# Tail of a routed feed-forward kernel: the threshold search with two small operations a bit, five bits in two pairs, and finding rounds of four tiles

## The chip, the cores and the metric

One core of one Trainium2 chip. The metric is the device time of one execution in microseconds (us), as the median of the timed runs.

## The reference, cut to what matters

A vision transformer, a memory layer and a routed feed-forward layer follow each other. The change is in the last one:

```python
T = Bn * Sn                                   # 64 * 229 = 14656 tokens of D = 128
logits = jnp.einsum('gsd,de->gse', xg, gate_w)          # E = 16 experts
probs = jax.nn.softmax(logits, axis=-1)
flat_probs = probs.transpose(2, 0, 1).reshape(En, T)
scores, tok_idx = jax.lax.top_k(flat_probs, cap)        # cap = T / E = 916 tokens an expert
toks = xf[tok_idx]
h = jax.nn.gelu(jnp.einsum('ecd,edh->ech', toks, w1) + b1[:, None, :])
y = jnp.einsum('ech,ehd->ecd', h, w2) + b2[:, None, :]
y = y * scores[..., None]
routed = jnp.zeros_like(xf).at[tok_idx.reshape(-1)].add(y.reshape(-1, Dn))
shared = jax.nn.gelu(xf @ sw1 + sb1) @ sw2 + sb2
out = (routed + shared).reshape(Bn, Sn, Dn)
```

## The kernel before, in words

The kernel is a row of phases; `tail_phase` is the last and the only one touched. It handles 32 pairs of sequences (PAIRS, the shared feed-forward on all tokens) and then 32 units (two for each of 16 experts, UNITS). Every engine runs one list of instructions written out by hand, with n from 0 to 63 for pair or unit, and semaphores between the lists.

**The main loop.** TensorE (PE) does for each n: `up(n+1)` (L1600 to L1612, four products of 458 columns into the banks U, each of them two passes of fp32) and `down(n)` (L1614 to L1625, 16 products of 128 columns into bank O). ScalarE (ACT) applies the gelu between them (L1714) and issues the output transfers of the shared part. VectorE (DVE) adds in `total_of(n)` (L1807 for pairs, L1815 and L1818 for units). GpSimd (POOL) adds the bias sb2 to h for each pair (L1784), and after that issues the indirect transfers.

**Routing.** At the start the DVE takes the softmax of the router's logits (L1932 to L1942, the exponential on ACT at L1735), PE turns the probabilities (L1642) and the DVE copies them to `prob` (L1948), 128 partitions of 1832 values, eight partitions for each expert. SP loads ten constants first (L1561), and PE, ACT, POOL and DVE each wait for all ten (`load` at 160) before their first work in the tail.

**The search.** The 916th largest probability of every expert is found bit by bit, 30 bits. For a bit, `search` (L1821 to L1828) forms a candidate `cand = thr | bit` (L1824) and counts the values at or over it (L1827, with an accumulator output); PE's `count` sums the counts of an expert's partitions into bank C (L1651); `settle` (L1830 to L1836) keeps the bit where the sum reaches 916 (L1832, L1835) and shifts the bit (L1836). Two bits go with each pair n = 1 to 15: PE issues up(n+1), count, down(n), count. Then `chosen` (L1842, L1843, a scan at L1848), `ranked` at n = 16 and `placed` at n = 17 turn the threshold into running counts `runx`, which SP writes to memory and reads back as `run64` (L1571, L1577).

**The finding.** For expert e, at n = 19 + e, `one_hot(e)` (L1890, L1893) builds rows that select for each slot its block of tokens; `find` (PE, L1664) multiplies them with the running counts, one round for two tiles of 120 slots, into bank C or X by turns; `tokens` (DVE, L1902 to L1913) subtracts the start from the slot in two steps, counts within the block (L1908, two tiles), and adds the token's base in two steps. There are four rounds an expert. PE's order is up(n+1), rounds 0 and 1, `turn_x` (L1633, from n = 30 on: the transposes of a later unit's tokens, in bank X, which wait for all rounds found so far), down(n), rounds 2 and 3. The DVE's order is tokens of rounds 0 and 1, total_of(n), tokens of rounds 2 and 3, one_hot of the next expert. So one_hot(e+1) stands behind the last round of e, and the first round of e+1 waits for it.

**Gather and scatter.** POOL gathers the rows of the first 12 experts (AHEAD) from `table`, eight transfers each (L1757), each pair of them as soon as its token indices are there. Then it runs `scatter(e)` for e = 0 to 15 (L1768, eight transfers with addition, the first four after y of unit 2e, the others after unit 2e+1), with four more gathers behind each of the first eight. The scatters of an expert wait until all those of the one before have landed. y has four buffers.

Of the kernel before, what the change touches and what calls it, by code (L numbers as in the profile page):

```python
# [12 lines left out]
F32 = mybir.dt.float32  # L13
BF16 = mybir.dt.bfloat16
I32 = mybir.dt.int32
# [869 lines left out]
WL = 2 * L  # L885
# [594 lines left out]
LAST_BIT = FIRST_BIT + BITS // 2 - 1  # L1480
# [4 lines left out]
def tail_phase(nc, g, A, out):  # L1485

    UNITS = 2 * E
    with ExitStack() as ctx:
        s = Sems(nc, ctx, "load ew0 ew1 gel_pad eb2 bias b_part up gelu down sum0 sum1 sent0 sent1 "
                 "r_max r_sub r_exp r_sum r_inv r_prob r_turn r_copy scored table "  # L1490
                 "t_set t_cand t_count t_total t_step t_thr t_bit t_gt t_tie t_pref t_off t_need t_sel t_run t_runoff "
# [24 lines left out]
        thr, bit, cand, step = (sb(n, [128, 1], I32) for n in ("thr", "bit", "cand", "step"))  # L1516
# [4 lines left out]
        local, inside, junk = sb("local", [XL, 2]), sb("inside", [XL, 2]), sb("junk", [XL, 2, BLK])  # L1521
# [17 lines left out]
        X, C = (ctx.enter_context(nc.psum_tensor(n, [128, 512], F32)) for n in ("z_X", "z_C"))  # L1539
        summed, sent = [s["sum0"], s["sum1"]], [s["sent0"], s["sent1"]]  # L1540
# [15 lines left out]
        with nc.Block() as block:  # L1556
            @block.sync
            def _(sp):
                for dst, src in ((sw1, "sw1"), (sw2, "sw2"), (sb1, "sb1"), (sb2, "sb2"), (eb1, "eb1"), (same, "same_expert"),
                                 (ahead, "ahead"), (slot, "slot"), (order, "order"), (base, "base")):  # L1560
                    sp.dma_start(dst[:], A[src]).then_inc(s["load"], 16)  # L1561
# [37 lines left out]
            def _(pe):  # L1599
                def up(n):  # L1600
# [4 lines left out]
                    for k in range(4):  # L1605
# [8 lines left out]
                def down(n):  # L1614
# [5 lines left out]
                    for t in range(4):  # L1620
# [4 lines left out]
                    mm.then_inc(s["down"], 1)  # L1625
# [27 lines left out]
                def find(e, r, turned):  # L1653
# [391 lines left out]
```

## Time and profile before

| | us |
|---|---|
| median of 3 runs | 3929.04 (3922.57 to 3930.95) |
| the profiled execution, its own time | 3925.95 |
| its span in the profile | 3924.1 |
| mean granted clock of TensorE | 0.949 of full speed |
| the tail | from 3223.7 to 3924.1 |

The profile is one execution. Times in rows are us from the start of its span. PE is the matmul, PEld the weight load, and a fp32 product shows as two rows. A row of the timeline gives start, length, engine, line, operation, tiles, number of instructions merged, and in brackets the idle time before it with what ended it. A merged row of matmuls ends some tenths after the next row starts, since the ends are modelled.

### The profile page before, as it was taken

What the parts mean: (1) busy time and instruction counts of PE and PEld (TensorE: products, weight loads), DVE (VectorE), ACT (ScalarE), POOL (GpSimd) and SP (SyncE); (2) the same over time, 40 slices, a digit from 0 to 9 for tenths busy, and PEclk for the clock granted to TensorE, in tenths of its full rate; (3) what the DMA queues carried; (4) which work ended last, traced back from release to release, by engine and by line L of the source; (5) the groups of instructions that cost most, each with busy time, mean ns of one, the idle gap of its engine ahead of it and who ended that gap; (6) DMA issues with size and microseconds to landing.
All of it is one profiled execution on the core that took longest, in us unless ns stands there. A gap on an engine that the chain in (4) does not pass through costs nothing. (4 is left out here: it accounts for less than half of the span.)

```text
span 3924.1 us, 88868 instructions
## 1 busy us (share of the span) xinstructions
PE 3456.2 (88%) x29756; PEld 2634.2 (67%) x29756; DVE 2496.5 (64%) x6387; ACT 1917.9 (49%) x3500; POOL 2285.1 (58%) x2633
## 2 busy tenths in 40 slices
PE   7899999889999889999988999996997879867973
PEld 4577787667877667787766777774445656645762
DVE  2267776567777556777655777666986878765110
ACT  0156666346666436666534666654653433211331
POOL 0356663756664475666365666455985643364876
PEclk9999999889999989999988999998998989988997
DMA  6856663146665036666214666501111222221432
GB/s 223 244 112 125 129 132 59 26 85 124 132 130 110 8 59 118 131 129 127 50 36 80 130 128 129 104 2 33 34 27 41 62 63 36 59 72 35 74 58 29
DMA packets 456054, 342.03 MB, mean 87 GB/s; under 512 B 70659, under 2 KB 440171, under 8 KB 455595
## 3 DMA queue, kind: packets, MB, share of 16 engines
q1 hardware_dynamic: 404419, 275.69, 35.9%
q10 hardware_dynamic: 24224, 46.44, 3.7%
q0 software_dynamic: 27136, 16.42, 3.1%
q8 instruction: 150, 2.46, 0.3%
q14 instruction: 125, 1.02, 0.1%
HBM read 227.69 MB, written 109.29 MB: 86 GB/s over the span
## 5 line engine op out<-in xcount | busy, mean ns | idle before, releaser
L730 DVE TENSOR_REDUCE a_neg_max<-a_S 99x4 f32<-99x788 f32 x1024 | 1003.6, 980 | 499.1 <-PE a_S L319 495.3
L528 ACT ACTIVATE a_shared<-a_St 99x792 f32<-99x792 f32 (+1 forms) x1024 | 850.3, 830 | 622.0 <-PE a_St L336 610.4
L319 PE MATMUL a_S<-a_k_st,a_q_st 96*99 96x197 bf16 x4096 | 546.8, 256 | 46.8 <-DVE a_neg_max L730 46.5
L319 PEld LDWEIGHTS a_S<-a_k_st,a_q_st 96*99 96x99 bf16 x4096 | 395.1, 127 | 265.3 <-DVE a_neg_max L730 226.6
L336 PE MATMUL a_St<-a_q_st,a_k_st 99*99 99x198 bf16 (+1 forms) x4096 | 523.4, 250 | 47.0 <-DMA a_q_st<-a_max_rows 31.8
L355 PE MATMUL a_O<-a_shared,a_v_aug 99*32 99x198 f32 (+1 forms) x8192 | 461.3, 337 | 0.6
L336 PEld LDWEIGHTS a_St<-a_q_st,a_k_st 99*99 99x99 bf16 (+1 forms) x4096 | 386.6, 125 | 76.8 <-DMA a_q_st<-a_max_rows 39.2
L355 PEld LDWEIGHTS a_O<-a_shared,a_v_aug 99*32 99x32 f32 (+1 forms) x8192 | 246.1, 109 | 82.9 <-ACT a_shared L528 1.3
L673 POOL TENSOR_TENSOR h<-h,a_rows 99x512 f32<-99x512 f32 x128 | 163.1, 1274 | 213.0 <-DVE a_shared L805 213.0
L641 POOL CAST a_max_parts<-a_neg_max 99x32 bf16<-99x32 f32 x128 | 26.8, 210 | 446.6 <-DVE a_neg_max L730 446.6
L659 POOL CAST a_parts<-a_q_k 128x792 bf16<-128x792 f32 x128 | 107.8, 843 | 306.7 <-issue 261.3
L468 PEld LDWEIGHTS a_O<-a_w,a_shared 128*99 128x99 f32 x2048 | 245.6, 168 | 46.3 <-issue 29.9
L468 PE MATMUL a_O<-a_w,a_shared 128*99 128x128 f32 x2048 | 267.7, 275 | 3.5 <-DVE h L828 3.5
L594 ACT ACTIVATE a_shared<-a_St,a_cols 128x396 f32<-128x396 f32 x256 | 150.9, 591 | 238.9 <-PE a_St L479 230.5
L1768 POOL DMA_INDIRECT out<-h,token x128 | 210.3, 1643 | 96.9 <-DVE h L1818 41.8
L828 DVE TENSOR_TENSOR h<-a_O,h 99x512 f32<-99x512 f32 x128 | 88.5, 692 | 226.7 <-PE a_O L468 226.7
L661 POOL TENSOR_TENSOR a_q_k<-a_q_k,a_parts 128x792 f32<-128x792 f32 x128 | 216.0, 1687 | 10.3
L665 POOL TENSOR_TENSOR a_parts<-a_q_k,a_parts 128x792 bf16<-128x792 f32 x128 | 215.7, 1685 | 10.3
L479 PE MATMUL a_St<-a_shared,a_w 128*128 128x396 f32 x512 | 208.3, 532 | 2.5 <-ACT a_shared L600 2.5
L1714 ACT ACTIVATE z_gel<-z_U,z_sb 128x458 f32<-128x458 f32 x128 | 80.5, 643 | 223.1 <-PE z_U L1611 188.0
L1815 DVE TENSOR_TENSOR h<-z_O,xT 120x512 f32<-120x512 f32 x32 | 22.1, 689 | 235.0 <-DMA out<-h,token 174.7
L1714 ACT ACTIVATE z_gel<-z_U,z_eb 128x458 f32<-128x458 f32 x128 | 81.5, 642 | 184.3 <-PE z_U L1611 169.6
(266 smaller groups left out, 7473.9 us busy)
## 6 DMA issues: line engine op xcount, KB each, us to landing
a_shared<-in_x ACTq DMA_DIRECT2D x64, 594.0 KB, 5.1
spill_q<-a_parts SPq DMA_DIRECT2D x384, 99.0 KB
spill_k<-a_parts SPq DMA_DIRECT2D x384, 99.0 KB
a_k_st<-spill_k SPq DMA_DIRECT2D x128, 297.0 KB
a_q_st<-spill_q SPq DMA_DIRECT2D x128, 297.0 KB
a_k_st<-spill_k SPq DMA_DIRECT2D x128, 198.0 KB
a_q_st<-spill_q SPq DMA_DIRECT2D x128, 198.0 KB
a_k_st<-spill_k SPq DMA_DIRECT2D x128, 99.0 KB
```

What stands on the lines that cost most here:

```text
L319: mm = nc.tensor.matmul(S[0:TC, j // 2, j % 2 * TB:j % 2 * TB + NTOK], q_st[p % 4][0:SPLIT, head, b * TB + c * TC:b * TB + (c + 1) * TC], ...
L336: mm = nc.tensor.matmul(St[0:keys, j // 2, j % 2 * TB:(j % 2 + 1) * TB], k_st[p][:, head, first:first + keys], q_st[p][:, head, b * TB:(b ...
L355: mm = nc.tensor.matmul(O[32 * j:32 * j + 32, half * TB:(half + 1) * TB], v_aug[p % 4][0:keys, 2 * b + c, half * 4 + j, :], probs[0:keys, ...
L468: mm = nc.tensor.matmul(O[0:TC, t * D:(t + 1) * D], gl[k % 2][:, h, t * TC:(t + 1) * TC], m.w2[:, h * D:(h + 1) * D], start=(h == 0), stop ...
L479: nc.tensor.matmul(St[:, h, 0:PW], m.w1[:, h * 128:(h + 1) * 128], m_yT[n % 2], start=True, stop=True).then_inc(s["m_fc1"], 1)
L528: nc.scalar.activation(probs[0:keys, u % 4, :].rearrange("p (x t) -> p x t", x=2), St[0:keys, :, 0:2 * TB], ACT.Exp).then_inc(s["probs"], 1)
L661: nc.gpsimd.tensor_tensor(q_k[:], q_k[:], parts[:, 0, :, :], ALU.subtract).then_inc(s["res"], 1)
L665: nc.gpsimd.tensor_tensor(parts[:, 2, :, :], q_k[:], parts[:, 1, :, :], ALU.subtract).then_inc(s["lo"], 1)
L673: nc.gpsimd.tensor_tensor(hp, hp, m.b2.unsqueeze(1).to_broadcast([TC, 4, D]), ALU.add).then_inc(s["m_bias"], 1)
L730: nc.vector.tensor_reduce(out.rearrange("p (x y) -> p x y", x=2), S[0:TC, :, 0:2 * TB].rearrange("p x (y t) -> p x y t", y=2)[:, :, :, 0:N ...
L1714: nc.scalar.activation(gel[n % 2][:, k, 0:WL], U[k][:, 0:WL], ACT.Gelu_apprx_tanh, bias=bias).then_inc(s["gelu"], 1)
L1768: nc.gpsimd.indirect_dma_start(out=out[:, :], out_offset=bass.IndirectOffsetOnAxis(g.token[0:n, e, k:k + 1].bitcast(U32), 0), in_=y[(2 * e ...
```

## The change

Four edits, all in `tail_phase`:

1. **Loads.** sw1, sb1 and sw2 come first, with a semaphore of their own (`load_w`, 48). PE and ACT wait for these three. The other seven (`load`, 112) are waited for by POOL before its biases, by PE after the turned probabilities, by ACT before the experts' first gelu, and by the DVE in n = 0, where the two operations on `base` now stand.
2. **Search.** `cand` starts as the top bit. After each count, `pre` is `cand` with the next lower bit set (SBUF to SBUF, one input). `settle` writes into bank X `fail`, which is this bit where the sum is under 916, and `cand` becomes `fail xor pre`. thr, bit and step are gone. 30 bits go with pairs 1 to 12, three in one pair and two in the next; PE cuts up and down into parts between the counts.
3. **After the search.** `ranked` and `placed` both stand in n = 13 on the DVE; PE's three small products stand between the halves of down(13) and down(14).
4. **Finding.** Expert e is found at n = 16 + e. A round has four tiles (both banks), two rounds an expert. Each tile has one product of 229 columns and two products of 2 columns that add up in PSUM what `tokens` added before. one_hot(e+1) stands between tokens(e, 0) and total_of(n). `find(e, 1)` now also waits for `copied`.

```diff
-LAST_BIT = FIRST_BIT + BITS // 2 - 1
+LAST_BIT = FIRST_BIT + 2 * (BITS // 5) - 1
-        thr, bit, cand, step = (sb(n, [128, 1], I32) for n in ("thr", "bit", "cand", "step"))
+        cand, pre = (sb(n, [128, 1], I32) for n in ("cand", "pre"))
+        fail = X[:, 0:1].bitcast(I32)
         def bits_of(n):
-            return [2 * (n - FIRST_BIT), 2 * (n - FIRST_BIT) + 1] if FIRST_BIT <= n <= LAST_BIT else []
+            if not FIRST_BIT <= n <= LAST_BIT:
+                return []
+            at = (n - FIRST_BIT) // 2 * 5
+            return [at, at + 1, at + 2] if (n - FIRST_BIT) % 2 == 0 else [at + 3, at + 4]
...
-                for dst, src in ((sw1, "sw1"), (sw2, "sw2"), (sb1, "sb1"), (sb2, "sb2"), (eb1, "eb1"), (same, "same_expert"),
-                                 (ahead, "ahead"), (slot, "slot"), (order, "order"), (base, "base")):
+                for dst, src in ((sw1, "sw1"), (sb1, "sb1"), (sw2, "sw2")):
+                    sp.dma_start(dst[:], A[src]).then_inc(s["load_w"], 16)
+                for dst, src in ((same, "same_expert"), (sb2, "sb2"), (ahead, "ahead"), (base, "base"), (slot, "slot"),
+                                 (order, "order"), (eb1, "eb1")):
                     sp.dma_start(dst[:], A[src]).then_inc(s["load"], 16)
...
                 def find(e, r, turned):
-                    wait(pe, s["token"], 4 * e + r - 1)
-                    if r % 2:
-                        wait(pe, s["copied"], turned)
-                    bank = (C, X)[r % 2]
-                    for t in range(2):
-                        k = 2 * (r % 2) + t
-                        at, n = (r // 2) * WL + XCOLS[k], XL
-                        mm = nc.tensor.matmul(bank[0:n, t * 256:t * 256 + RUN], hot[e % 2][:, at:at + n],
-                                              run64[:, e, :], start=True, stop=True)
+                    wait(pe, s["token"], 4 * e + 2 * r)
+                    wait(pe, s["copied"], turned)
+                    for k in range(4):
+                        at = r * WL + XCOLS[k]
+                        bank, to = (C, X)[k // 2], k % 2 * 256
+                        one = hot[e % 2][:, at:at + XL]
+                        nc.tensor.matmul(bank[0:XL, to:to + BLK], one, run64[:, e, 0:BLK], start=True, stop=True)
+                        for part in range(2):
+                            mm = nc.tensor.matmul(bank[0:XL, to + BLK:to + BLK + 2], one,
+                                                  run64[:, e, BLK + 2 * part:BLK + 2 * part + 2],
+                                                  start=(part == 0), stop=(part == 1))
...
+                    if len(bits) == 3:
+                        count(bits[0])
+                        up(n + 1)
+                        count(bits[1])
+                        down(n, range(3))
+                        count(bits[2])
+                        down(n, range(3, 4))
+                        continue
+                    if len(bits) == 2:
+                        up(n + 1, range(2))
+                        count(bits[0])
+                        up(n + 1, range(2, 4))
+                        down(n, range(1))
+                        count(bits[1])
+                        down(n, range(1, 4))
+                        continue
...
                 def search(k):
-                    wait(dve, s["t_thr"], k)
-                    wait(dve, s["t_bit"], k)
-                    nc.vector.tensor_tensor(cand[:], thr[:], bit[:], ALU.bitwise_or).then_inc(s["t_cand"], 1)
                     wait(dve, s["t_cand"], k + 1)
                     wait(dve, s["t_total"], k)
                     nc.vector.tensor_scalar(gt, prob, cand[:].bitcast(F32), None, ALU.is_ge, ALU.add,
                                             accum_out=cnt[:]).then_inc(s["t_count"], 1)
+                    if k + 1 < BITS:
+                        nc.vector.tensor_single_scalar(pre[:], cand[:], 1 << (BITS - 2 - k),
+                                                       ALU.bitwise_or).then_inc(s["t_pre"], 1)
                 def settle(k):
                     wait(dve, s["t_total"], k + 1)
-                    nc.vector.scalar_tensor_tensor(out=step[:], in0=C[:, 0:1], scalar=float(CAP), in1=bit[:],
-                                                   op0=ALU.is_ge, op1=ALU.mult).then_inc(s["t_step"], 1)
+                    nc.vector.tensor_scalar(fail, C[:, 0:1], float(CAP), float(1 << (BITS - 1 - k)), ALU.is_lt,
+                                            ALU.mult).then_inc(s["t_step"], 1)
                     wait(dve, s["t_step"], k + 1)
-                    nc.vector.tensor_tensor(thr[:], thr[:], step[:], ALU.bitwise_or).then_inc(s["t_thr"], 1)
-                    nc.vector.tensor_single_scalar(bit[:], bit[:], 1, ALU.logical_shift_right).then_inc(s["t_bit"], 1)
+                    wait(dve, s["t_pre"], min(k + 1, BITS - 1))
+                    nc.vector.tensor_tensor(cand[:], fail, (pre if k + 1 < BITS else cand)[:],
+                                            ALU.bitwise_xor).then_inc(s["t_cand"], 1)
...
                 def tokens(e, r):
+                    for k in range(2):
+                        nc.vector.tensor_tensor(local[:, 2 * k:2 * k + 2], slot[:, 4 * r + 2 * k:4 * r + 2 * k + 2],
+                                                two[k][0:XL, :, BLK], ALU.subtract).then_inc(s["local"], 1)
+                    for k in range(4):
+                        dve.wait_ge(s["local"], 2 * n_r + 1 + k // 2)
+                        nc.vector.tensor_scalar(junk[:, k, :], two[k // 2][0:XL, k % 2, 0:BLK], local[:, k:k + 1], None,
+                                                ALU.is_le, ALU.add, accum_out=inside[:, k:k + 1]).then_inc(s["inside"], 1)
+                    for k in range(2):
+                        dve.wait_ge(s["inside"], 4 * n_r + 2 * k + 2)
+                        nc.vector.tensor_tensor(g.token[:, e, 4 * r + 2 * k:4 * r + 2 * k + 2], two[k][0:XL, :, BLK + 1],
+                                                inside[:, 2 * k:2 * k + 2], ALU.add).then_inc(s["token"], 1)
...
                     if e is not None:
-                        for r in range(2):
-                            tokens(e, r)
+                        tokens(e, 0)
+                        if e + 1 < E:
+                            one_hot(e + 1)
                     total_of(n)
                     if e is not None:
-                        for r in range(2, 4):
-                            tokens(e, r)
-                    if expert_of(n + 1) is not None:
-                        one_hot(n + 1 - FIRST_EXPERT)
+                        tokens(e, 1)
+                    if expert_of(n + 1) == 0:
+                        one_hot(0)
```

## Rows read from the trace of the kernel before

**Rows 1.** Windows: stretch, length, busy PE PEld DVE ACT POOL, PEclk, DMA share.

```profile
3253.00:3370.00 117.00, 105.94 (x651) 79.71 (x650) 104.36 (x187) 36.90 (x58) 35.59 (x29) 1.00 0.24 37
3399.00:3587.00 188.00, 132.65 (x679) 100.48 (x680) 113.10 (x483) 34.23 (x56) 102.07 (x96) 0.85 0.26 67
```

**Rows 2.** Timeline, POOL: last gather before scatters; scatters of expert 0, 2.

```profile
3559.46 0.98 POOL L1757 DMA_INDIRECT xT<-table,token  x1 [0.30 <-issue]
3587.69 1.67 POOL L1768 DMA_INDIRECT out<-h,token  x1 [27.24 <-DVE h L1818]
...
3643.36 1.64 POOL L1768 DMA_INDIRECT out<-h,token  x1 [0.30 <-issue]
```

**Rows 3.** Timeline: one round pair of the finding, PE and DVE.

```profile
3552.46 0.41 PE L1664 MATMUL z_C<-z_prob_run,z_wide 64*120 64x233 bf16 x2
...
3556.33 0.16 DVE L1913 TENSOR_TENSOR token<-z_X,z_inside 120x2 int32<-120x2 f32 x1
...
3557.13 1.17 DVE L1893 SCALAR_TENSOR_TENSOR z_wide<-z_order,z_last,z_wide 64x922 bf16<-64x922 f32 x1
...
3558.40 0.38 PE L1664 MATMUL z_C<-z_prob_run,z_wide 64*120 64x233 bf16 x2 [2.06 <-issue]
```

**Rows 4.** The chain of waits near 3635 us: PE at full clock.

```profile
3635.52 3.08 PE z_U L1611 x8
...
3639.00 3.50 PE z_O L1623 x32
```

**Rows 5.** Waits in 3396 to 3560 us: us in total, times, longest.

```profile
DVE z_ys L1807 <- remote: 18.1, 3, 6.7
```

**Rows 6.** Timeline: one and a half bits of the search.

```profile
3264.33 0.38 PE L1651 MATMUL z_C<-z_cnt,z_same 128*128 128x1 f32 x2 [0.23 <-DVE z_wide L1827]
...
3264.75 0.16 DVE L1832 SCALAR_TENSOR_TENSOR z_step<-z_C,z_bit 128x1 int32<-128x1 f32 x1 [0.48 <-PE z_C L1651]
...
3265.47 2.12 DVE L1827 TENSOR_SCALAR_CACHE_REDUCE z_wide<-z_prob_run,z_cand 128x1832 f32<-128x1832 f32 x1
...
3267.73 0.30 PE L1651 MATMUL z_C<-z_cnt,z_same 128*128 128x1 f32 x2
...
3268.28 2.50 POOL L1784 TENSOR_TENSOR h<-h,z_sb 115x512 f32<-115x512 f32 x2 [4.95 <-DVE z_ys L1807]
3268.30 1.27 DVE L1835 TENSOR_TENSOR z_thr<-z_thr,z_step 128x1 int32<-128x1 int32 x1
```

**Rows 7.** Timeline: PE at the first and at the last of the 30 counts.

```profile
3253.21 0.28 PE L1651 MATMUL z_C<-z_cnt,z_same 128*128 128x1 f32 x2
...
3370.21 0.38 PE L1651 MATMUL z_C<-z_cnt,z_same 128*128 128x1 f32 x2 [1.40 <-DVE z_wide L1827]
```

**Rows 8.** Groups of the tail: the two small VectorE operations with two SBUF inputs.

```profile
L1824 DVE TENSOR_TENSOR z_cand<-z_thr,z_bit 128x1 int32<-128x1 int32 x30 | 17.0, 566 | 3.1
...
L1835 DVE TENSOR_TENSOR z_thr<-z_thr,z_step 128x1 int32<-128x1 int32 x30 | 12.5, 418 | 1.0
```

**Rows 9.** Timeline, routing: start us, us, engine, line, operation, tiles, count.

```profile
3223.86 0.06 DVE L1920 MEMSET z_zero<- 128x1 f32 x1
...
3230.80 1.21 DVE L1932 TENSOR_REDUCE z_max<-logits 115x64 f32<-115x1024 f32 x1
...
3238.75 5.04 PE L1611 MATMUL z_U<-xT,z_sw 128*128 128x458 f32 x8 [2.23 <-ACT z_gel L1714]
...
3246.52 0.16 DVE L1824 TENSOR_TENSOR z_cand<-z_thr,z_bit 128x1 int32<-128x1 int32 x1
```

**Rows 10.** Timeline: from the search to the first gather.

```profile
3399.10 0.38 PE L1664 MATMUL z_C<-z_prob_run,z_wide 64*120 64x233 bf16 x2 [3.59 <-DVE z_wide L1893]
...
3402.19 1.25 POOL L1757 DMA_INDIRECT h<-table,token  x1 [34.22 <-issue]
```

**Rows 11.** Timeline: eight PE passes of 16 columns each.

```profile
3199.38 0.89 PE L1341 MATMUL y_L<-y_router,y_zs 128*115 128x16 f32 x8
```

**Rows 12.** Timeline: a down at the lower clock.

```profile
3530.64 6.50 PE L1623 MATMUL z_O<-z_sw,z_gel 128*115 128x128 f32 x32
```

More of the change, by code:

```diff
@@ L1599, in _, with up @@
             def _(pe):
-                def up(n):
+                def up(n, parts=range(4)):
                     u = n - PAIRS
@@ L1604, in up @@
                         wait(pe, s["copied"], u + 1)
-                    for k in range(4):
+                    for k in parts:
                         wait(pe, s["gelu"], 4 * (n - 1) + k + 1)
@@ L1612, in up, with down @@
                                          stop=True).then_inc(s["up"], 1)
-                def down(n):
+                def down(n, tiles=range(4)):
                     u = n - PAIRS
@@ L1619, in down @@
                     wait(pe, s["gelu"], 4 * (n + 1))
-                    for t in range(4):
+                    for t in tiles:
                         to = O[n % 2][0:rows, t * D:(t + 1) * D]
@@ L1624, in down @@
                                                   start=(k == 0), stop=(k == 3))
-                    mm.then_inc(s["down"], 1)
+                    if tiles[-1] == 3:
+                        mm.then_inc(s["down"], 1)
                 def turn_x(u, found):
@@ L1679, in _ @@
                         pe.wait_ge(s["r_copy"], 4)
-                    if bits:
-                        count(bits[0])
+                        pe.wait_ge(s["load"], 112)
                     if e is not None:
-                        for r in (0, 1):
-                            find(e, r, turned)
-                            found += 1
+                        find(e, 0, turned)
+                        found += 2
                     if PAIRS <= n + 2 < PAIRS + UNITS:
@@ L1688, in _ @@
                         turned += 1
-                    down(n)
-                    if bits:
-                        count(bits[1])
+                    down(n, range(2))
                     if n == LAST_BIT + 1:
@@ L1700, in _ @@
                         nc.tensor.matmul(C[:, 0:1], ahead[:], run[:, W - 1:W], start=True, stop=True).then_inc(s["t_runoff"], 1)
+                    down(n, range(2, 4))
                     if e is not None:
-                        for r in (2, 3):
-                            find(e, r, turned)
-                            found += 1
+                        find(e, 1, turned)
+                        found += 2
             @block.scalar
@@ L1896, in tokens @@
                 def tokens(e, r):
-                    n_r = 4 * e + r
-                    bank = (C, X)[r % 2]
-                    two = bank[:].rearrange("p (t n) -> p t n", n=256)
+                    n_r = 2 * e + r
+                    two = [bank[:].rearrange("p (t n) -> p t n", n=256) for bank in (C, X)]
                     dve.wait_ge(s["found"], n_r + 1)
-                    wait(dve, s["token"], n_r)
-                    nc.vector.tensor_tensor(local[:], slot[:, 2 * r:2 * r + 2], two[0:XL, :, BLK],
-                                            ALU.subtract).then_inc(s["local"], 1)
@@ L1916, in _ @@
                 for p in range(2):
                     nc.vector.memset(gel[p][:, :, WL:], 0.0).then_inc(s["gel_pad"], 1)
-                nc.vector.memset(thr[:], 0).then_inc(s["t_set"], 1)
-                nc.vector.memset(bit[:], 1 << (BITS - 1)).then_inc(s["t_set"], 1)
+                nc.vector.memset(cand[:], 1 << (BITS - 1)).then_inc(s["t_cand"], 1)
                 nc.vector.memset(zero[:], 0.0).then_inc(s["t_set"], 1)
-                dve.wait_ge(s["load"], 160)
-                nc.vector.tensor_copy(runx[:, :, BLK + 1], base[:]).then_inc(s["b_part"], 1)
@@ L1924, in _ @@
-                dve.wait_ge(s["b_part"], 1)
-                nc.vector.tensor_tensor(runx[:, :, BLK + 3], base[:], runx[:, :, BLK + 1], ALU.subtract).then_inc(s["t_final"], 1)
                 def wide_b(a):
@@ L1950, in _ @@
                 dve.wait_ge(s["r_copy"], 4)
-                dve.wait_ge(s["t_set"], 3)
+                dve.wait_ge(s["t_set"], 1)
                 search(0)
```

38 lines of the change are left out of this document (17 added, 21 removed).

## The prediction, made before the changed kernel ran

> **What bounds the kernel now.** I read the page first, then the tail in windows, then the chain of waits backwards from its end, and the timeline wherever the chain changes engine. Only the tail is touched, so the question is what sets its 700 us.
>
> The end hangs on POOL. From the scatters of expert 2 at 3643.36 the chain goes through POOL's transfers alone up to the end of the span at 3924.1: 280.7 us of work that the change leaves as it is. Between expert 0's scatters at 3587.69 and expert 2's lie 55.7 us; in steady state an expert with its four gathers takes 20.6 us (7.7 for four scatters, twice, and 5.2 for gathers), so 14.5 us of these are waits for y. The last gather before them was issued at 3559.46: POOL is idle for 27 us and waits for y of unit 0 [rows 2]. So the end moves with the first y, and gains up to 14.5 us more if units 0 to 3 follow each other closely.
>
> The first y hangs on the finding, which has 188 us at a granted clock of 0.85 with PE busy for 133 [rows 1]. The timeline shows a ring: rounds 2 and 3 on PE at 3552.46, their tokens on the DVE till 3556.49, one_hot till 3558.30, and only then the next expert's rounds at 3558.40, though PE has been free for 2.06 us [rows 3]. From n = 30 on, turn_x waits for tokens as well. At full clock PE's own work for n is 3.1 + 3.5 us [rows 4]; 13 experts' iterations took (3587.69 - 3399.10) / 13 = 14.5 us each. Three times the DVE and ACT also wait together for something that the trace doesn't name: 18.1 us in all on the DVE, up to 6.7 each [rows 5].
>
> Ahead of that is the search: from one count to the next 3.40 us where an up lies between [rows 6], 117.0 us for 29 intervals [rows 7]. The window's granted clock is 1.00 and the DVE is busy for 104 of 117 us [rows 1]. Here the DVE's small operations stall: L1835 takes 1.27 us in place of 0.16, from the start of a POOL addition to its end [rows 6]. In sum the two small operations with two SBUF inputs cost 29.5 us for 60, where 60 at 0.16 make 9.6 [rows 8]: 19.9 us lost.
>
> **Part 1, loads.** The DVE's first reduction starts at 3230.80, but its memsets end at 3223.92 [rows 9]; nothing but the ten loads lies between. Its part moves 6.9 us. PE still waits for three of the ten loads, so it starts sooner by part of that; up(0) then up(1) at half clock, in front of the turned probabilities, hold back part of the gain (up(1) took 5.04 us [rows 9]). The bounds are 2 and 6.9; I take 4, nearer to PE's end, since PE is last in this chain. The moved waits cost nothing: all ten loads have landed by 3230.8 now [rows 9] and are first asked for after 3240. The DVE's two operations on base (0.2 us each) come behind search(0), while PE does down(0); if that cover went they would cost 0.4 us once.
>
> **Part 2, search.** First, count(0) no longer stands behind up(2): -3.1 us [rows 4]. Then the ring of one bit. Now it is 0.42 (count to settle), 0.72 (settle, thr, cand, to the scan), 2.18 (scan to the next count) [rows 6]. The change takes one of the dependent operations and the pair of waits out, so 0.72 becomes 0.39, and the ring 2.99. `pre` runs in the 0.5 us in which the DVE waits for the count; it costs 0.15 us where there is no such cover. That the DVE writes a PSUM operand is in no row. Nearest is L1832, which reads PSUM and takes 0.16 like the others; I take 0.16, with 0.10 and 0.35 as ends (-2 and +6 us for 30 bits). The xor has one SBUF input, so I take it as free of POOL's hold, as L1832 was.
>
> PE lies between the counts with 3.08 (an up), 2.63 (three quarters of a down), 2.41, 2.41 and 2.63 us. Only the first is over the ring: 3.40. The DVE's total_of, 0.69 us once a pair, adds 0.3 of it once in five bits (the other time it hides under the 3.40). Five bits: 3.40 + 4 x 2.99 + 0.3 = 15.7; 29 intervals: 6 x 15.7 - 3.0 = 91. Against 117.0: -26.
>
> Together the search ends 4 + 3.1 + 26 = 33 us sooner. The stretch from there to the first find holds the same chain of scans, two PE products, the write and the read back. PE's halves of down fit into the scans of 4.0 and 2.1 us. One total_of (0.7 us) goes from the chain: -0.6. SP's queue keeps its order of writes and reads. So the first find comes at 3399.10 - 33.7 = 3365.4 and the first gather near 3370 instead of 3402.19 [rows 10].
>
> The Trainium skill speaks against a PSUM operand: VectorE: DVE Perf Modes, section on the TRN2 errata, gives VectorE a fixed 58 cycles from SBUF and 120 from PSUM. By that the xor would cost 65 ns more, an estimate of 2 us for 30 bits. Here L1832 with a PSUM input shows 0.16 us, like L1824 unstalled.
>
> **Part 3, finding.** One_hot(e+1) (1.87 us) now stands under down(n), out of the ring. Tokens for four tiles: from 3.4 us (two rounds of 1.65) to 0.35 (two subtractions), 4 x 0.38 (counts), 0.3 (two additions), 2.2 us. The find itself grows. Four products of 233 columns take 0.54 us [rows 3]; eight of 2 columns with their weight loads come on top. The nearest row is eight passes of 16 columns in 0.89 us [rows 11]: I take 0.75, so 1.3 us a find, with 0.9 and 1.7 as ends (32 finds: -13 and +13 us).
>
> PE per iteration: up 3.27, find 1.3, down 3.68, find 1.3 = 9.55 us (the 3.08 and 3.50 of [rows 4], with an estimated 0.2 each for the change of product). The DVE needs 2 x 2.2 + 1.87 + 0.7 = 7.0 and is never last: tokens(e, 1) hide under the up, tokens(e, 0) and one_hot under down. So PE bounds, with no gaps, and the clock should come near 1.00. Fourteen such iterations: 133.7. For n = 30 and 31 turn_x stands behind the tokens: 12.3 us each. Then turn_x, down(32) and y: 5.3. From 3365.4 that gives 3529. I keep the unnamed waits, four of 5 us, as PE has no slack for them: first y at 3549, instead of 3587.69, although 16 iterations lie ahead of it and not 13. POOL's 96 gathers, 1.33 us each, would end by 3370 + 128 = 3498; not a bound.
>
> **Sum.** First y -38.7; POOL's waits behind it -14.5, since units now follow each 7.0 us with no find between, under POOL's 7.7 [rows 2, 4]: -53 us. The profiled execution took 3925.95, 1.9 over its span and 3.1 under the median. 3925.95 - 53 = 3873; I say 3871, between this and the same sum with one unnamed wait less.
>
> **Rivals.** (a) The finding keeps a ring: the unnamed waits stay on every second iteration, or the small products cost 0.2 us each, and an iteration takes 12 us. Then 16 x 2.45 = 39 us come back: 3910. For it: three such waits in 160 us now. Against: the DVE has a third less to issue. (b) All goes well: no unnamed waits, the find at 0.9 us: -20 and -13 against the forecast, 3838. (c) The other side: PE loses its clock in the finding. At the lower clock down takes 6.5 us [rows 12] and an up up to 6.0, a find 2.6: 17.7 an iteration, 16 x 8.15 = 130 us more, 4001. It decides from 9.55 + 53/16 = 12.9 us an iteration on. For it: 0.85 in that window [rows 1]. Against: it fell behind idle stretches of 6 to 8 us, and PE's idle time mostly goes. (d) The five bits in two pairs don't shorten the ring, as xor or the PSUM write waits for POOL as thr did: +20 us of [rows 8], 3891.
>
> **How the numbers follow.** Forecast 0.62, (a) 0.11, (b) 0.12, (c) 0.04, (d) 0.11. The unknown costs added in squares give about 17 us either way around 3871. The range of 3842 to 3904 holds the forecast, (d) and much of (b); (a) and (c) are left out. A measurement of this kernel can tell about 0.2%, 8 us, from no change. Slower takes (c) and little else: 0.04. Within 8 us needs (a) in a stronger form: 0.02. Faster 0.94.
>
> **What would show it.** First find near 3365; 29 intervals of count in about 91 us, 3.0 between most; no 128x1 operation of the DVE over 0.3 us in the search; bank C and X products in bursts of 12 taking 1.3 us, PE without gaps between them and a granted clock near 1.00; the scatters of expert 0 near 3549 and those of expert 2 some 41 us later, then 281 us to the end. I am wrong if the first y is later than 3580, or if POOL's part behind it isn't 322 us.

## The result and the profile after

| | before | changed |
|---|---|---|
| median of 13 runs, us | 3932.16 (3920.45 to 3945.95) | 3903.31 (3888.05 to 3924.36) |
| the profiled execution | 3925.95 | 3896.24 |
| its span | 3924.1 | 3894.5 |

The ratio is 0.9923, with a 95% interval of 0.9906 to 0.994, so the change is some 30 us faster. The forecast of 3871 lay 55 us under the profiled execution of before and 58 under the median that the prediction had. The profiled execution took 3896.24 where the sum said 3873. The direction is right, the size about half. (The median of before is 3.1 us over the three runs that the prediction had.)

Windows of the changed kernel (stretch, length, busy PE PEld DVE ACT POOL, PEclk, DMA share, GB/s), the search and the finding, answering to [rows 1]:

```profile
3245.00:3335.00 90.00, 88.05 (x519) 64.20 (x517) 79.59 (x156) 30.84 (x48) 29.88 (x24) 1.00 0.29 39
3365.00:3540.00 175.00, 148.15 (x903) 110.80 (x903) 90.33 (x387) 35.00 (x56) 101.01 (x96) 0.86 0.29 73
```

The search is short and at full clock. The finding is not: 175 us, with a granted clock of 0.86 and PE idle for 26.9 of them.

**Up to the search**, timeline, answering to [rows 9]:

```profile
3222.95 0.22 DVE L1460 COPY logits<-y_L 115x64 f32<-115x64 f32 x1 [3.36 <-PE y_L L1341]
...
3226.03 1.22 DVE L1946 TENSOR_REDUCE z_max<-logits 115x64 f32<-115x1024 f32 x1
...
3230.28 8.72 PE L1617 MATMUL z_U<-xT,z_sw 128*128 128x458 f32 x16 [7.38 <-DMA z_sw<-in_sw]
...
3241.74 2.12 DVE L1847 TENSOR_SCALAR_CACHE_REDUCE z_wide<-z_prob_run,z_cand 128x1832 f32<-128x1832 f32 x1
```

The DVE's first reduction follows its memsets at once. The first scan of the search starts at 3241.74; before, the first candidate was formed at 3246.52 [rows 9] and its scan began 0.2 us later. This execution reached its tail 2.4 us later (the last copy of the logits at 3222.95; before at 3220.51), so the routing is 7.4 us shorter (5.0 + 2.4). PE is last: it waits 7.38 us for its loads, then up(0) and up(1) run in one piece of 8.72 us. Before, up(1) waited 2.23 us for ACT in between [rows 9].

**The search**, one bit in the timeline, answering to [rows 6]:

```profile
3248.73 0.38 PE L1658 MATMUL z_C<-z_cnt,z_same 128*128 128x1 f32 x2
...
3249.15 0.17 DVE L1855 TENSOR_SCALAR z_X<-z_C 128x1 int32<-128x1 f32 x1 [0.41 <-PE z_C L1658]
3249.35 0.16 DVE L1859 TENSOR_TENSOR z_cand<-z_X,z_pre 128x1 int32<-128x1 int32 x1
...
3251.72 0.38 PE L1658 MATMUL z_C<-z_cnt,z_same 128*128 128x1 f32 x2
```

From 3248.73 to 3251.72, count to count, are 2.99 us, as the prediction has it. The groups of the three small operations (busy us, mean ns of one), answering to [rows 8]:

```profile
L1855 DVE TENSOR_SCALAR z_X<-z_C 128x1 int32<-128x1 f32 x30 | 4.9, 162 | 7.4 <-PE z_C L1658 7.4
L1859 DVE TENSOR_TENSOR z_cand<-z_X,z_pre 128x1 int32<-128x1 int32 x29 | 4.6, 157 | 1.2 <-DVE z_X L1855 0.2
L1850 DVE TENSOR_SCALAR z_pre<-z_cand 128x1 int32<-128x1 int32 x29 | 4.3, 148 | 0.0
```

`fail` reads and writes PSUM in 162 ns, the xor with a PSUM input takes 157, `pre` with SBUF alone 148, and none of the 89 took over 0.17 us, so none was held by POOL. The first and the last count, answering to [rows 7]:

```profile
3245.35 0.28 PE L1658 MATMUL z_C<-z_cnt,z_same 128*128 128x1 f32 x2
...
3335.01 0.38 PE L1658 MATMUL z_C<-z_cnt,z_same 128*128 128x1 f32 x2 [0.19 <-DVE z_wide L1847]
```

29 intervals take 89.7 us instead of 117.0.

**Behind the search**, timeline of the DVE, then POOL's bias in the same time:

```profile
3344.00 2.90 DVE L1880 SCALAR_TENSOR_TENSOR z_wide<-z_run,z_need,z_wide 128x1832 f32<-128x1832 f32 x1
3346.93 4.92 DVE L1883 TENSOR_TENSOR_SCAN z_run<-z_wide 128x1832 f32<-128x1832 f32 x1
```

```profile
3343.71 4.32 POOL L1807 TENSOR_TENSOR h<-h,z_sb 115x512 f32<-115x512 f32 x2 [8.53 <-DVE z_ys L1830]
```

These two took 2.13 and 3.97 us before, with nothing on POOL beside them. Now two additions of the bias, from 3343.71 to 3348.03, lie over the whole of the first and over the first 1.1 us of the second. The two are 1.7 us longer in all, and all of it is on the chain. That POOL holds them, as it held the small operations of [rows 6], is read from these times alone. The first find and the first gather, answering to [rows 10]:

```profile
3365.46 0.28 PE L1670 MATMUL z_C<-z_prob_run,z_wide 64*120 64x229 bf16 x1 [1.68 <-DVE z_wide L1917]
...
3369.39 1.25 POOL L1780 DMA_INDIRECT h<-table,token  x1 [8.53 <-DVE token L1933]
```

3365.46 where 3365.4 was forecast.

**The finding and POOL**, answering to [rows 2]:

```profile
3523.04 1.29 POOL L1780 DMA_INDIRECT xT<-table,token  x1 [0.30 <-issue]
3571.69 1.67 POOL L1791 DMA_INDIRECT out<-h,token  x1 [47.37 <-DVE h L1841]
...
3613.77 1.64 POOL L1791 DMA_INDIRECT out<-h,token  x1 [0.30 <-issue]
```

The gathers end at 3523.04 and POOL idles for 47.37 us: y comes at 3571.69, not at 3549. Behind it all is as forecast: 42.1 us from expert 0's scatters to expert 2's (41.2 said), then 280.7 us to the end, to a tenth the figure of before. So the miss of the sum, 22.7 us, lies between the first find and the first y.

The chain of waits in the finding has these pieces, start and length in us:

```profile
3373.85 7.67 another core or an unknown queue
...
3404.25 3.71 another core or an unknown queue
...
3412.86 6.70 another core or an unknown queue
...
3467.36 8.82 another core or an unknown queue
...
3489.03 7.38 another core or an unknown queue
...
3510.36 6.05 another core or an unknown queue
```

Nine pieces (three of 2.9 us and less left out here) make 46.2 us. The same view of the kernel before, over its whole finding:

```profile
3410.50 4.25 another core or an unknown queue
...
3427.87 6.73 another core or an unknown queue
...
3480.00 5.14 another core or an unknown queue
...
3517.38 6.46 another core or an unknown queue
```

Four pieces make 22.6 us. What such a piece looks like from PE (timeline):

```profile
3467.93 0.45 PE L1672 MATMUL z_C<-z_prob_run,z_wide 64*120 64x2 bf16 x2
3468.94 0.29 PE L1670 MATMUL z_X<-z_prob_run,z_wide 64*120 64x229 bf16 x1 [0.56 <-issue]
...
3470.37 0.16 PE L1672 MATMUL z_X<-z_prob_run,z_wide 64*120 64x2 bf16 x1 [1.13 <-issue]
...
3471.07 0.16 PE L1672 MATMUL z_X<-z_prob_run,z_wide 64*120 64x2 bf16 x1 [0.33 <-issue]
3471.78 6.07 PE L1617 MATMUL z_U<-xT,z_sw 128*128 128x458 f32 x8 [0.55 <-issue]
```

A find's products are normally 0.15 us or less apart; here they come up to 1.3 us apart, with idle time of kind "issue". The DVE and ACT wait in the same time. On POOL the gathers follow each other there every 1.3 us. The up behind it takes 6.07 us where 3.3 is normal, and this part is the clock, as its own window shows (columns as above):

```profile
3471.78:3477.85 6.07, 6.07 (x8) 2.52 (x8) 1.65 (x8) 1.48 (x3) 2.16 (x3) 0.54 0.14 34
```

So a stall costs twice: PE idles, and then it works for a while at the lower of its two levels (1.2 and 2.4 GHz). The waits of the DVE in 3366 to 3580 us (us in total, times, longest) show why [rows 5] said too little:

```profile
DVE z_local L1925 <- DMA spill_k<-a_parts: 37.8, 8, 7.7
...
DVE z_ys L1830 <- remote: 18.8, 5, 7.7
```

The "remote" line is hardly longer than the 18.1 us before. But `spill_k` is a transfer of an earlier phase that had long landed, so that line too is a wait whose end the trace can't name. In the finding before it was 3.1 us.

### The profile page after: what moved, and what is told of

Same layout as the page of the kernel before. It is cut to its first block and busy times, and to the rows that moved or that the text cites. A ratio compares the mean times of both kernels' runs of the same rounds, so it can differ in the third digit from the quotient of the medians.

```text
span 3894.5 us, 89214 instructions
## 1 busy us (share of the span) xinstructions
PE 3477.2 (89%) x30012; PEld 2650.4 (68%) x30012; DVE 2445.2 (63%) x6227; ACT 1919.0 (49%) x3500; POOL 2285.7 (59%) x2633
## 5 line engine op out<-in xcount | busy, mean ns | idle before, releaser
L468 PEld LDWEIGHTS a_O<-a_w,a_shared 128*99 128x99 f32 x2048 | 243.7, 167 | 45.5 <-issue 28.9
```

Of the source, the lines that this page charges most:

```text
L468: mm = nc.tensor.matmul(O[0:TC, t * D:(t + 1) * D], gl[k % 2][:, h, t * TC:(t + 1) * TC], m.w2[:, h * D:(h + 1) * D], start=(h == 0), stop ...
```

## The experiments

The yardstick is **F**, the time from expert 0's find to expert 14's: 14 iterations, read from one profile of each run. An iteration without any stall is 4.58 + 4.20 = 8.8 us in the changed kernel, so F = 123.3 is a finding without stalls. The changed kernel of the result has 174.1, the kernel before 192.8. Three theories for the 50 us of difference: (A) POOL's gathers hold PE back; (B) PE's instructions, 12 products a find, are what runs short; (C) the output transfers of the shared part collide with something. A fourth came up behind the first runs: (D) the stalls hang on the chip.

Runs made together share a chip and its runs of the kernel before; the chips are called P to T, in the order of the runs.

### Chip P: four edits

**Gathers late.** POOL issues no gather before the tokens of expert 13.

```diff
+                pool.wait_ge(s["token"], 56)
                 for e in range(AHEAD):
                     gather(e)
```

> POOL waits for the tokens of experts 0 to 13 before it issues its first gather, so no gather runs beside the finding; nothing else is changed. Theory A (a continuous stretch of POOL's gathers holds PE's instructions and semaphore updates back, which makes the stalls of the finding): the stretches between finds of 6.5 to 11.3 us vanish while no gather runs, an iteration takes 8.8 us, and the find of expert 13 starts near 3365.5 + 13 x 8.8 = 3480 instead of 3531; the end comes later, since 96 gathers of 1.33 us then stand behind the finding: first y's scatters near 3480 + 9 + 128 = 3617 or later, a time of about 3940 to 3950. Theory B (PE's own instructions, 12 products a find, are what can't be delivered in time) and theory C (the output transfers of the shared part) leave the stalls where they are: the find of expert 13 near 3531 and a time near 3990.

**Gathers paced.** POOL waits for an expert's gathers to land before the next expert's.

```diff
                 for e in range(AHEAD):
                     gather(e)
+                    for m in range(2):
+                        pool.wait_ge(x_in[e][m], 64)
```

> After the eight gathers of each of the first 12 experts POOL waits until they have landed before it issues the next. Theory A: the gathers no longer stand in one queue for tens of us, the stalls of the finding shrink to a third or less, an iteration takes about 9.2 us, the first scatter comes near 3535 instead of 3571.7, and the kernel takes 3860 to 3875 us against 3903 of the changed kernel. Theories B and C: stalls stay, first scatter near 3572 to 3580, 3903 to 3912 us.

**Short sends.** From pair 14 on each output transfer carries one row; their number stays.

```diff
-                        k = TL - c
+                        k = TL - c if n < 14 else 1
```

> From pair 14 on the shared part's output is sent as one row instead of 114 or 115 (this part of the output is left out), same number of transfers. Theory C (the output transfers of the shared part collide with the gathers and hold PE back): the stalls vanish or halve, iteration 8.8 to 10 us, first scatter 3520 to 3540. Theories A and B: the sum of the slow steps stays within a quarter of what it was (46 us in unnamed waits), first scatter 3565 to 3575, about 3900 us.

**Four products a find.** On the DVE the second subtraction and second addition of before come back, for two tiles at a time (not in the cut below).

```diff
-                        nc.tensor.matmul(bank[0:XL, to:to + BLK], one, run64[:, e, 0:BLK], start=True, stop=True)
-                        for part in range(2):
-                            mm = nc.tensor.matmul(bank[0:XL, to + BLK:to + BLK + 2], one,
-                                                  run64[:, e, BLK + 2 * part:BLK + 2 * part + 2],
-                                                  start=(part == 0), stop=(part == 1))
+                        mm = nc.tensor.matmul(bank[0:XL, to:to + RUN], one, run64[:, e, :], start=True, stop=True)
```

> Each tile of the finding is one product of 233 columns as in the kernel before, and the parts of the sums are added on the DVE again (four more small operations a round of four tiles); the rounds of four tiles stay. Theory B (the number of PE instructions makes the stalls): the unnamed waits fall from 46 us to the 22 of the kernel before, the first scatter comes 15 to 25 us sooner, 3880 to 3890 us. Theory A: the waits stay, the DVE's extra 0.6 us a round costs up to 1 us an iteration, 3900 to 3915 us.

| chip P | us (runs) | ratio to before | F |
|---|---|---|---|
| kernel before | 3916.0 (8) | 1 | |
| gathers late | 3949.7 (3) | 1.0083 (1.0055 to 1.0110) | 123.2 |
| gathers paced | 3859.0 (4) | 0.9858 (0.9829 to 0.9887) | 124.9 |
| short sends | 3850.6 (2) | 0.9832 (0.9798 to 0.9866) | 123.3 |
| four products | 3846.4 (4) | 0.9819 (0.9794 to 0.9844) | 113.0 |

None of the four shows a stall in F. Each theory got what it wanted, and so none is told apart: a yardstick was missing, for the changed kernel itself was not run on this chip. The kernel before was also 16 us quicker than in the result.

### Chip Q: the unchanged kernels again

> The changed kernel, nothing else done to it. If the stalls of the finding belong to this program (theories A, B and C alike), they come again: find of expert 0 to find of expert 14 in about 174 us with ten or more steps between finds over 6.5 us, and a ratio to the kernel before of 0.992. If they come and go from one execution or one chip to another, as the four kernels before this one leave possible since each of them lost them, this run too may show 123 to 135 us and a ratio of 0.983 to 0.987.

> The kernel before, profiled again. If its unnamed waits (22.6 us on the chain in the finding) belong to the program, find of expert 0 to the last of its finds takes 220 us again and its first scatter stands 189 us behind the first find. If they come and go, the first scatter comes up to 25 us sooner after the first find.

The changed kernel took 3904.0 us (6 runs; before 3937.5; ratio 0.9913, 0.9884 to 0.9941), F = 170.8. The kernel before has F = 192.4 and its first scatter 188.2 us behind its first find; these are those of the result within 3%. Its time, 3933.7 us (8 runs), is that of the other runs of before. So the stalls come again, on this chip.

### Chip R: yardstick, two repeats, and both edits together

> The changed kernel once more, on the same chip as the three runs behind it. It stalled on two chips; the four edited kernels did not, but they ran together on another chip, and the kernel before was 16 us quicker there. Theory D (the stalls hang on the chip, not on the program): wherever this one stalls, the three behind it stall too, and all take 3895 to 3905 us; where it doesn't, it takes 0.983 to 0.985 of the kernel before. Theories A and B: this one stalls, some 50 us in the finding, 0.992, and the edited ones don't.

> The paced gathers again, beside the changed kernel. Theory A: no steps over 6.5 us between finds up to expert 13, 0.985 of the kernel before and at least 20 us under the changed kernel of the same chip. Theory D: it stalls as much as the changed kernel does here, or as little, and the two are within 8 us.

> Four products a find, again, beside the changed kernel. Theory B (PE's instructions are what runs short): no stalls, 0.982 of the kernel before, and at least 25 us under the changed kernel. Theories A and D: where the changed kernel stalls this one does too, and it lies within 10 us of it (an iteration is 0.6 us shorter, 10 us over 16).

> Four products a find and paced gathers together, the candidate for the fastest. Theory A: no stalls, and POOL's paced gathers (12.8 us an expert, 154 us) instead of PE set the first scatter, so it equals the paced kernel within 5 us, near 0.984. Theory D on a chip that stalls: stalls stay, near 0.99.

| chip R | us (6 runs each) | ratio to before | F |
|---|---|---|---|
| kernel before | 3939.0 (11 runs) | 1 | |
| changed | 3902.5 | 0.9912 (0.9878 to 0.9946) | 177.6 |
| gathers paced | 3898.6 | 0.9904 (0.9876 to 0.9931) | 161.8 |
| four products | 3903.4 | 0.9898 (0.9869 to 0.9926) | 171.5 |
| both | 3877.9 | 0.9831 (0.9797 to 0.9866) | 142.5 |

The same two programs that had F = 124.9 and 113.0 on chip P stall here by 37 and 58 us. Theory B falls: a third of the find's instructions doesn't free it (171.5 against 113.0 unstalled), and the time stays that of the changed kernel. Pacing an expert at a time takes 16 us off F in one profile, which was the fastest execution of its six (3886.3), and nothing that the times can tell. So the gathers needn't stand in one unbroken row: eight at a time, each eight landed before the next, still leave 37 us. Both together are faster than the changed kernel beyond either interval, and still stall by some 29 us. Why the two edits do more together than the sum of each, the runs don't tell; each is one profile.

### Chip S: yardstick, late gathers, short sends, and plain transfers

The new kernel takes the gathers out of POOL. SP issues 96 ordinary transfers of the same size, with the same waits:

```diff
+                            sp.dma_start(x[e][0:XL, k, :], g.table[k * XL:(k + 1) * XL, :]).then_inc(x_in[e][r // 2], 16)
...
-                for e in range(AHEAD):
-                    gather(e)
```

> The changed kernel, the yardstick for the three kernels behind it on this chip. Where it stalls: find of expert 0 to find of expert 14 in 171 to 178 us, 48 to 54 us over the 123.2 of 14 unstalled iterations. Where it doesn't: 123 to 125 us.

> No gather before the tokens of expert 13. On a chip where the changed kernel stalls: theory A (the gathers bring the stalls) 123 to 128 us from the first find to that of expert 14; theory B (PE's instructions) and theory C (output transfers) 165 us or more.

> From pair 14 on the shared part's output is sent as one row a transfer (that part of the output is left out). On a chip where the changed kernel stalls: theory C 123 to 135 us from the first find to that of expert 14, theory A 160 us or more.

> The 96 gathers beside the finding become 96 plain transfers of the same size from SP's queue, of fixed rows of the table (the rows of the chosen tokens are left out, so the output of 12 experts is that of other rows). On a chip where the changed kernel stalls: if the stalls come from POOL's own part in a gather, or from how its transfers are described, 123 to 130 us from the first find to that of expert 14; if they come from the bytes moved, 150 us or more. The end comes sooner by up to 15 us, as POOL's gathers are gone ahead of the scatters.

The yardstick itself: 3859.0 us (2 runs, 3856.3 to 3861.6; before 3921.6, ratio 0.9857, 0.9808 to 0.9906), F = 123.3. The unchanged program doesn't stall on this chip, so the other three (F = 124.9, 123.3, 124.9; 3947.8, 3857.4 and 3847.2 us) tell nothing apart, except that theory D holds in this form: a chip, in its session, stalls this program or doesn't. Chip P was most likely such a chip too, with nothing to cure: three of its four versions stall on other chips in the same 14 iterations. Windows of the yardstick's finding:

```profile
3381.00:3505.00 124.00, 123.79 (x903) 95.91 (x904) 90.26 (x387) 35.76 (x56) 93.04 (x89) 1.00 0.38 98
```

PE is busy for 123.79 of 124 us at full clock. One find (timeline):

```profile
3389.99 0.31 PE L1670 MATMUL z_C<-z_prob_run,z_wide 64*120 64x229 bf16 x1
...
3390.92 3.75 PE L1629 MATMUL z_O<-z_sw,z_gel 128*115 128x128 f32 x32
```

A find takes 0.93 us on PE (3389.99 to 3390.92). The first y:

```profile
3536.67 1.67 POOL L1791 DMA_INDIRECT out<-h,token  x1 [21.37 <-DVE h L1841]
```

The first y comes 155.5 us behind the first find (3381.21), against 206.2 in the result. Set beside the window of the result, this one splits the 51 us of stalls in two. PE idles for 26.9 us instead of 0.2, and the same 903 products keep it busy for 148.2 us instead of 123.8, at a clock of 0.86 instead of 1.00. In the seven stretches of the result's window that show a granted clock of 0.50 PE is busy for 42.0 us, which at full clock would be 21. So of the 51 us some 21 are the lower clock behind the pauses.

### Chip T: the four again, and this chip stalls

> The changed kernel as the yardstick again: on a fifth or sixth chip it either stalls (171 to 178 us from the first find to that of expert 14, some 3900 us) or doesn't (123 to 125 us, some 3860 us). The kernel before should take 3930 to 3940 us in the first case and 3915 to 3922 in the second.

> If this chip stalls: theory A (it needs POOL's gathers) 123 to 128 us from the first find to that of expert 14; theories B and C 165 us or more. If it doesn't, 123 to 125 us and nothing is told apart.

> If this chip stalls: theory C (it needs the output transfers) 123 to 135 us, theory A 160 us or more. That part of the output is left out.

> If this chip stalls: 123 to 130 us if it needs the software gathers, 150 us or more if the bytes of the transfers, from whatever queue, bring it. The rows of the chosen tokens of 12 experts are left out and fixed rows of the table fetched in their place.

| chip T | us (runs) | ratio to before | F |
|---|---|---|---|
| kernel before | 3930.3 (5) | 1 | |
| changed | 3909.0 (3) | 0.9947 (0.9925 to 0.9970) | 174.8 |
| short sends | 3903.9 (3) | 0.9933 (0.9901 to 0.9965) | 177.6 |
| gathers late | 3968.9 (2) | 1.0102 (1.0064 to 1.0140) | 124.9 |
| plain transfers | 3850.6 (2) | 0.9801 (0.9742 to 0.9859) | 123.3 |

Windows from the first find to expert 14's: changed, short sends, gathers late (with the stretch behind it), plain transfers. Columns as above; the last two are DMA share and GB/s.

```profile
3378.00:3553.00 175.00, 146.96 (x900) 108.52 (x901) 90.27 (x386) 33.88 (x56) 100.17 (x96) 0.88 0.28 72
```

```profile
3376.00:3553.00 177.00, 146.24 (x895) 111.50 (x896) 89.96 (x386) 34.12 (x55) 101.17 (x96) 0.87 0.22 53
```

```profile
3367.00:3492.00 125.00, 125.00 (x897) 97.08 (x898) 89.77 (x386) 35.38 (x55) 0.26 (x1) 0.99 0.18 48
3492.00:3580.00 88.00, 21.46 (x125) 18.34 (x126) 8.41 (x39) 4.32 (x7) 67.62 (x68) 0.60 0.24 58
```

```profile
3362.00:3486.00 124.00, 123.86 (x905) 95.97 (x905) 89.58 (x386) 35.88 (x56) 0.00 (x0) 1.00 0.40 102
```

Theory C has little left: with the output transfers cut to a row, DMA moves 53 GB/s instead of 72 and F is what it was. Theory A holds. Without gathers there is no stall on a chip where the unchanged program has 51 us of them, and PE keeps its full clock. And it isn't the bytes: with plain transfers in their place DMA moves 102 GB/s, with PE busy for 123.86 of 124 us. In the late kernel the stall comes with the gathers. In the 88 us behind 3492 POOL issues 68 of them and PE is busy for 21 us at 0.60. Part of that is a plain wait for the gathered rows, so the same 88 us of the same program on chip S have to stand beside it:

```profile
3505.00:3593.00 88.00, 63.57 (x404) 49.88 (x404) 16.65 (x60) 25.50 (x42) 67.56 (x68) 0.87 0.30 79
```

With the same 68 gathers, PE there does 404 products and not 125. In the 88 us of chip T, PE and ACT's last output transfer show (timeline):

```profile
3518.37 0.77 ACTq L1751 DMA_DIRECT2D out<-z_ys  x2
...
3541.55 1.00 PE L1640 MATMUL z_X<-ident,h 120*128 120x120 f32 x4 [27.07 <-issue]
3542.34 5.73 PE L1629 MATMUL z_O<-z_sw,z_gel 128*115 128x128 f32 x30
3549.91 0.37 PE L1629 MATMUL z_O<-z_sw,z_gel 128*115 128x128 f32 x1 [1.83 <-issue]
3553.41 0.37 PE L1629 MATMUL z_O<-z_sw,z_gel 128*115 128x128 f32 x1 [3.13 <-issue]
...
3588.43 0.92 PE L1617 MATMUL z_U<-h 128*128 128x458 f32 x1 [2.64 <-issue]
3591.24 0.92 PE L1617 MATMUL z_U<-h 128*128 128x458 f32 x1 [1.88 <-issue]
```

The same program on chip S, same place:

```profile
3512.17 1.03 PE L1640 MATMUL z_X<-ident,h 120*128 120x120 f32 x4 [6.29 <-DMA h<-table,token]
3512.99 6.21 PE L1629 MATMUL z_O<-z_sw,z_gel 128*115 128x128 f32 x32
```

There PE waits 6.29 us for the gathered rows and then runs its 32 products in one piece; on chip T it stands for 27.07 us with nothing named, does 30 of 32, and then idles for 1.83 and 3.13 us before one product each. From 3556 to 3608 it issues one product every 2 to 4 us, while POOL issues a gather every 1.3 us; the last gather is issued at 3615.17, and at 3629.69 PE runs as usual. No output transfer is issued behind 3518.37, and from 3525 to 3610 DMA carries nothing but the gathers and three packets of instructions, at 54 GB/s. The stall goes on all the same, and that is the end of theory C. It also delays the first y: 271.9 us behind the first find, against 249.3 for this program on chip S. So a stall needs two things: POOL's gathers, and a chip that is prone. What lies between a gather and PE's issue isn't shown; the plain transfers change who issues, the queue and the form of the transfer all at once. Nor is it shown whether it is the chip, its place or that hour: each chip was used in one sitting only.

## Why the prediction was right in sign and wrong in size

**Part 1, loads: right, too small.** "I take 4", with bounds of 2 and 6.9. Measured 7.4, past the upper bound. "Up(0) then up(1) at half clock ... hold back part of the gain" was counted as a loss, but up(1) had stood in front of them before as well, behind a wait of 2.23 us for ACT [rows 9]. That wait went with the earlier softmax, so this stretch got shorter: from the start of up(0) to the turned probabilities it took 8.6 us instead of 13.1.

**Part 2, search: right.** Ring 2.99 (2.99 said; its 2.18 from scan to count isn't the 2.26 of [rows 6], but the scans later in that trace have it), the first count 2.9 us sooner behind its scan (3.1 said), 29 intervals 89.7 us (91 said). The PSUM operand costs nothing of note. The Trainium skill (VectorE: DVE Perf Modes, the section on the TRN2 errata) has 58 fixed cycles for a source in SBUF and 120 for one in PSUM. By an estimate from that, PSUM costs 65 ns more an operation; here the three groups are 162 and 157 ns with PSUM against 148 without, so 9 to 14 ns, and the measurement decides. "After-search chain -0.6" was wrong: it is 30.4 us where it was 28.9 [rows 7, 10]. The prediction looked at POOL's hold on the small operations and not at the long ones, on which POOL's later biases now fall. The first find at 3365.46 hits 3365.4 by luck, because the errors cancel: -3.4 (loads), -1.3 (intervals), +0.2 (first count), +2.2 (the chain behind the search) and +2.4 of a tail that began later make 0.1.

**Part 3, finding: the step that failed.** The sum of PE's work was too large, if anything: 9.55 us an iteration said, 8.8 measured, since a find takes 0.93 and not 1.3 (the eight 2-column products add 0.4 us in all). What failed is "I keep the unnamed waits, four of 5 us", together with "the clock should come near 1.00". Those two made 20 us; F is 50.8 over the unstalled 123.3. Of these, PE's idle time makes 26.9 us, not far over the 20 said. The other half, 24.4 us, was put at nothing: it is PE's longer busy time, some 21 us of it by the lower clock behind the pauses (0.86 over the stretch). The source of the 20 was too small as well. It took the DVE's three "remote" waits of 18.1 us [rows 5], where the chain of waits had 22.6; that chain has 46 us in the changed kernel. And the prediction carried them over as a fixed charge in time. They come with POOL's gathers, 96 of them before and after, issued over 157 us then and 154 now, so the gathers didn't get denser. What changed is that PE has no idle time left in the loop in which a pause could pass unseen. That this is why the same gathers cost more is argued, not shown: there is no profile of the kernel before on a chip that doesn't stall. Its times allow it: it is some 16 us slower on the stalling chips, the changed kernel 44 to 50. First y 3571.69 against 3549, 22.7 us: that is nearly the whole miss of 23 (+31 for the stalls, -8 for PE's sum). Rival (a) had the nearest account ("the unnamed waits stay on every second iteration", 12 us each; 174.1 / 14 = 12.4 measured), with a chance of 0.11. Its 3910 is 7 us over the median.

**Part 4, POOL behind the first y: right.** 42.1 and 280.7 us, -13.6 of the waits (14.5 said).

**Rivals.** (c), the clock, didn't come on its own: in the finding it is 1.00 on chip S, and 0.99 and 1.00 on chip T with the gathers late or replaced. It falls to 0.86 to 0.88 where stalls make PE idle, and there it makes some 21 of the 51 us. (d) didn't come: the small operations of the search took 0.15 to 0.17 us. (b), no unnamed waits and a find of 0.9, is what chip S shows: 3859.0 us against 3921.6, -63 by the medians (two runs; the ratio's interval allows -37 to -75). Its 3838 went from a base that itself contains stalls; the kernel before is at 3916 and 3922 on P and S and at 3930 to 3939 on the stalling chips. A change has two values here: some -60 us on a chip that doesn't stall, -21 to -37 on one that does.

## What to carry to other kernels

Where the chain of waits has pieces that the trace can't name, don't carry them over as a constant: see what runs beside every one of them, and ask whether the slack that swallowed it goes and what the clock does behind it. Run the unchanged kernel beside each experiment; four edits "removed" 50 us on a chip where, as far as the later runs tell, nothing had to be removed. Of the versions run, four products a find with gathers paced by expert is the fastest of those that leave nothing out on a stalling chip (0.9831, below both kernels there), and four products alone took 0.9819 on one that showed no stall.

## What the runs showed of the hardware

- On three of five chips (that of the result not counted), POOL's indirect gathers beside PE's work came with pauses in PE's issue of up to 9 us at a time on the chain, 48 to 54 us in 14 iterations of this loop. On a fourth the same program ran without a gap, and on the fifth its edited versions did. Plain transfers of the same size from SP brought no pause on the one stalling chip on which they were tried.
- Gathers behind each other are enough: with them alone, in the late kernel, PE once stood for 27.07 us with nothing named and then issued one product every 2 to 4 us.
- A good part of what these pauses cost was the clock behind them: the same 903 products kept PE busy for 148.2 us at a granted clock of 0.86, and for 123.8 at 1.00.
- Eight products of 2 columns with their weight loads add 0.4 us to four of 229 columns.
- A VectorE operation that reads and writes one element a partition in PSUM takes 162 ns; SBUF to SBUF 148.
